# A wait for the project product between GpSimd's scatters

## The chip, the core and the metric

The kernel runs on one core of a Trainium2 chip. The metric is the device time of one execution in microseconds (us); three executions of the kernel before were timed. Every time that is read from a trace comes from one further, profiled execution.

## The reference

Per image, 14 x 14 patches are projected to 128 features, a class token and positions are added, and 128 text tokens are appended: 325 tokens of 128 features, for 128 images. On the layer-normed tokens runs an attention-like block (cumulative sums of phase-rotated values, written here as masked score products), whose result goes through a gate and the product with `Wo`, and is added back:

```
return x + total / norm @ Wo + bo
```

Then a second layer norm, and a mixture of experts: 64 experts, top 2 per token, at most 256 tokens per expert in order of arrival, and a shared expert beside them:

```
pos = cumulative count of the token's expert - 1
buf = zeros((E, CAP, d)).at[flat_e, pos].set(x_pairs, mode='drop')
y = silu(buf @ w1) * (buf @ w3) @ w2
return (shared + routed)
```

## The kernel before

The 128 images are worked on in 64 pairs. Each engine has its own program, written out in order: a loop over turns `k`, in which it does one stage of several pairs (`p1` is the pair of the turn before, `p2` the one before that, and so on). Semaphores count up once per pair and stage, and `wait_ge(S["pe_wo"], n)` waits until stage `pe_wo` has been done for `n` pairs. There is no scheduler: the order on an engine is the order of the calls in its `body(k)`, and the engine stands still while a wait is not met.

A pair goes through these steps, with the lines of the profile:

- TensorE (PE) makes the tokens (L919) and turns them over to rows; VectorE (DVE) takes their statistics and, in `scaled`, writes the variance `ve` (L1342). GpSimd (POOL) raises it to the power -1/2 in `rstd` (`rs`, L591). DVE's `bias_scale` waits for that and writes `nb` (L1348), with which ScalarE (ACT) normalizes both the new pair (`xh`, L739) and, for an earlier pair, the input of the second norm (`xs`, L726). One `rs` of 12 columns serves two pairs: six columns of the first norm of one pair, six of the second norm of the pair two before it.
- On DVE, behind `nb` in the same turn, stand the masks, the counts of the experts, the slots (`slot`, L1448, the row of `slot_rows` to which each token goes), and last `tot` (L1470), the gated sum.
- PE's `project` (L1078) is the first call of PE's next turn: it multiplies `tot` with `Wo` and counts up `pe_wo`. DVE's `second_rows` (L1499) waits for it and writes `h2`, from which the second norm's statistics are taken, which go into the same turn's `ve`.
- POOL scatters each token of a pair twice (top 2) to `slot_rows` in HBM, by 12 indirect DMAs (L605): `scatter(p8, part)` issues two for one of six parts. In its turn `k` it waits for the slots of pair `k - 8`, scatters parts 0 to 2, computes `rs` of pair `k - 4`, and scatters parts 3 to 5.

After the loop, the 64 experts run over what lies in `slot_rows`; SyncE (SP) waits for all scatters ahead of that. POOL then adds the results into `out_rows` (L639).

The turns of the engines are not in step by number. POOL's turn `k` holds `rs` of pair `k - 4`, whose variance DVE makes in its turn `k - 3`. The `project` of pair `k - 5` stands in PE's turn `k - 2`.

Of the kernel before, what the change touches and what calls it, by code (L numbers as in the profile page):

```python
# [141 lines left out]
def first(pair):  # L142
    return pair.c == 0


def steps(body, begin, end):

    for k in range(begin, PAIRS + end):
        body(Pair(k))
# [43 lines left out]
def expert_pairs(eng, body):  # L193

    for n in range(E // 2):
        body(Experts(n // 4, n % 4))


def wait_expert(eng, sem, pair, back=0, each=1):

    n = pair.number() + (1 - back)
    if not pair.fixed() or n > 0:
        eng.wait_ge(sem, n * each)
# [10 lines left out]
def program(nc, t, out, slots_d):  # L214
    ctx = ExitStack()
    with ctx:
# [3 lines left out]
        def sem(name):  # L220
            return ctx.enter_context(nc.semaphore(name))
# [7 lines left out]
        def cst(name, p=128):  # L229
            a, b = CONST[name]  # L230
            return const[0:p, a:b]
# [168 lines left out]
        S = {n: sem(n) for n in names}  # L400
# [13 lines left out]
        def first_columns(eng, n):  # L414

            b0, count = CHUNKS[n]
            return eng.tensor_copy(cols[:, b0:b0 + count, :], raw[:, 0, :].rearrange("p (t b) -> p b t", b=P)[:, b0:b0 + count, :])
# [155 lines left out]
        @block.gpsimd  # L573
        def _(pool):
            g = nc.gpsimd
            g.memset(neg_half[:, :], -0.5)
            g.memset(freq[:, :], 0.0).then_inc(s_pre_p, 1)
            pool.wait_ge(s_xin[0], 16 * 2 * C)
            first_columns(g, 2).then_inc(S["a_d2"], 1)
            g.memset(init_rows[:, :, 0:E_COL], 0.0).then_inc(s_pre_p, 1)  # L580
            g.memset(init_rows[:, :, E_COL:P_COL], -1.0)
            g.memset(init_rows[:, :, P_COL:T_COL], 0.0)
            pool.wait_ge(s_const, 16)
            g.tensor_copy(init_rows[:, :, T_COL], cst("empty")).then_inc(s_pre_p, 1)
            pool.wait_ge(s_pre_p, 3)

            def rstd(q):

                pool.wait_ge(S["v_ve"], q.count())
                half = 0 if q.runs() else 2 * NT  # L590
                g.tensor_tensor(out=rs[:, q.u, half:], in0=ve[:, q.u, half:], in1=neg_half[:, half:], op=ALU.pow).then_inc(S["p_rs"], 1)  # L591

            def ready(q):

                if first(q):
                    pool.wait_ge(s_init, 16 * (SLOTS // 1024 + 1))

                pool.wait_ge(S["v_slot"], q.count())

            def scatter(q, part):  # L600

                i = part % NT
                nt = TILES[i][1]
                for r in range(TOPK):
                    g.indirect_dma_start(  # L605
                        out=slots_d, out_offset=bass.IndirectOffsetOnAxis(
                            ap=slot[0:nt, q.x, r, part:part + 1], axis=0),
                        in_=xs[0:nt, q.x, part, :], in_offset=None, bounds_check=SLOTS - 1,
                        oob_is_err=False).then_inc(s_scat[q.x], 16)

            def body(k):
                p4 = k.back(4)
                p8 = k.back(8)
                if p8.runs():
                    ready(p8)
                    scatter(p8, 0)
                    scatter(p8, 1)
                    scatter(p8, 2)
                if p4.runs(BEHIND):
                    rstd(p4)  # L620
                if p8.runs():
                    scatter(p8, 3)
                    scatter(p8, 4)
                    scatter(p8, 5)
            steps(body, 4, 8)

            for u in range(2):
                pool.wait_ge(s_store[u], 16 * NT * (PAIRS // 2))
            pool.wait_ge(l_store, 16 * NT * len(LATER))

            last_row = pool.to_reg(TOKENS + SPARE - 1)

            def add(q):

                for e, ready in enumerate(("e_ya", "e_yb")):
                    wait_expert(pool, X[ready], q)
                    wait_expert(pool, e_add[e], q, 1, 32)
                    for m in (2 * e, 2 * e + 1):
                        g.indirect_dma_start(  # L639
                            out=out, out_offset=bass.IndirectOffsetOnAxis(ap=etok[:, q.load, m:m + 1], axis=0),  # L640
                            in_=ysum[:, q.load, m, :], in_offset=None, bounds_check=last_row,
                            compute_op=ALU.add).then_inc(e_add[e], 16)

            expert_pairs(pool, add)
            for e in range(2):
                pool.wait_ge(e_add[e], (E // 2) * 32)
# [1116 lines left out]
```

## Time and profile before

| what | value |
|---|---|
| three timed executions | 1828.45, 1853.2, 1863.95 us |
| their median | 1853.2 us |
| the profiled execution: first to last instruction | 1823.6 us |
| its own time outside of that span | not given; the lowest timed run is 4.85 us above the span, the median 29.6 us |
| PE, DVE, ACT, POOL busy | 1534.0, 1421.6, 1256.5, 1226.0 us |
| the loop, first `rs` behind a scatter to the last `rs` | 132.9 to 1514.8 us |
| scatters (L605) | 768 |

A busy time is the sum over an engine's instructions. The granted clock is 1.00 where TensorE had its full rate and 0.50 where it had half. "issue" as a releaser means that the trace shows nothing that the engine waited for, "remote" that the semaphore's update is seen later than the end that the trace has for any instruction that could have made it.

### The profile page before, as it was taken

What the parts mean: (1) busy time and instruction counts of PE and PEld (TensorE: products, weight loads), DVE (VectorE), ACT (ScalarE), POOL (GpSimd) and SP (SyncE); (2) the same over time, 40 slices, a digit from 0 to 9 for tenths busy, and PEclk for the clock granted to TensorE, in tenths of its full rate; (3) what the DMA queues carried; (4) which work ended last, traced back from release to release, by engine and by line L of the source; (5) the groups of instructions that cost most, each with busy time, mean ns of one, the idle gap of its engine ahead of it and who ended that gap; (6) DMA issues with size and microseconds to landing.
All of it is one profiled execution on the core that took longest, in us unless ns stands there. A gap on an engine that the chain in (4) does not pass through costs nothing.

```text
span 1823.6 us, 30829 instructions
## 1 busy us (share of the span) xinstructions
PE 1534.0 (84%) x9237; PEld 1158.6 (64%) x9237; DVE 1421.6 (78%) x5705; ACT 1256.5 (69%) x2195; POOL 1226.0 (67%) x973
## 2 busy tenths in 40 slices
PE   2888998999899999888989898999889975676672
PEld 1566776777676767656767666677667764554552
DVE  3477997999797988777888888889888975587661
ACT  2897997988788878777878787889878851111110
POOL 1025776777676767666667676777667767488887
PEclk9899999999999999999999999999999998899886
DMA  9965666666666666556555655566656221476653
GB/s 182 229 138 120 138 139 125 123 121 124 102 117 100 117 101 106 96 103 103 95 101 104 108 102 102 101 111 105 103 103 103 63 59 40 96 116 109 98 88 35
DMA packets 267117, 197.21 MB, mean 108 GB/s; under 512 B 65464, under 2 KB 246437, under 8 KB 266953
## 3 DMA queue, kind: packets, MB, share of 16 engines
q1 hardware_dynamic: 210120, 174.84, 50.2%
q0 software_dynamic: 51200, 17.87, 8.4%
q10 hardware_dynamic: 5633, 2.56, 0.7%
q8 instruction: 74, 1.21, 0.3%
q14 instruction: 90, 0.74, 0.2%
HBM read 86.24 MB, written 85.39 MB: 94 GB/s over the span
## 4 chain that ended last, share of the span: by engine, by line
PE 40%; ACT 22%; issue 11%; POOL 9%; another core or an unknown queue 8%; DVE 7%; DMA 3%; SPq 0%; ACTq 0%; POOLq 0%; DVEq 0%
POOL out_rows L639 6%; PE bank L919 5%; PE bank L999 5%; ACT img L656 5%; ACT xh L739 4%; PE bank L1087 3%; PE bank L982 3%; POOL slot_rows L605 3%; PE bank L946 2%; PE bank L1018 2%; PE bank L1078 2%; ACT xs L726 2%; ACT kq L793 2%; ACT kq L792 2%
## 5 line engine op out<-in xcount | busy, mean ns | idle before, releaser
L605 POOL DMA_INDIRECT slot_rows<-xs,slot x768 | 874.1, 1138 | 284.5 <-issue 247.3
L656 ACT ACTIVATE img<-img 84x980 f32<-84x980 f32 x190 | 339.6, 1788 | 14.8 <-DMA img<-in_x 7.2
L591 POOL TENSOR_TENSOR rs<-ve,neg_half 128x12 f32<-128x12 f32 (+1 forms) x66 | 150.3, 2277 | 234.4 <-DVE ve L1342 232.8
L919 PE MATMUL bank<-img,w_tok 126*128 126x392 f32 (+1 forms) x640 | 228.7, 505 | 27.9 <-DMA img<-img 23.3
L639 POOL DMA_INDIRECT out_rows<-img,etok x128 | 198.7, 1552 | 64.0 <-issue 35.0
L919 PEld LDWEIGHTS bank<-img,w_tok 126*128 126x128 f32 (+1 forms) x640 | 124.0, 195 | 113.3 <-issue 23.3
L982 PEld LDWEIGHTS bank<-pos_a,v 128*128 128x128 f32 x768 | 145.4, 198 | 54.0 <-issue 10.8
L982 PE MATMUL bank<-pos_a,v 128*128 128x325 f32 (+2 forms) x768 | 163.8, 351 | 6.1 <-issue 3.8
L726 ACT ACTIVATE xs<-h,nb,rs 128x128 f32<-128x128 f32 x384 | 154.0, 481 | 3.0 <-DVE nb L1348 3.0
L739 ACT ACTIVATE xh<-h,nb,rs 128x128 f32<-128x128 f32 x384 | 154.0, 480 | 1.3 <-DVE nb L1348 1.3
L1499 DVE TENSOR_TENSOR h<-bank,hbo 128x768 f32<-128x768 f32 x64 | 61.1, 955 | 114.6 <-remote 103.3
L999 PE MATMUL bank<-a_t,v 128*128 128x325 f32 (+2 forms) x768 | 149.9, 344 | 0.0
L999 PEld LDWEIGHTS bank<-a_t,v 128*128 128x128 f32 x768 | 126.4, 192 | 21.6 <-issue 0.4
L880 ACT ACTIVATE img<-bank 128x256 f32<-128x256 f32 x32 | 12.3, 384 | 174.0 <-PE bank L1191 129.2
L1219 PE MATMUL bank<-img,mate 128*128 128x128 f32 x504 | 77.2, 316 | 65.2 <-issue 65.2
L1219 PEld LDWEIGHTS bank<-img,mate 128*128 128x128 f32 x504 | 71.0, 225 | 72.2 <-issue 72.1
L1078 PEld LDWEIGHTS bank<-wo,tot 128*128 128x128 f32 x768 | 90.5, 191 | 32.0 <-issue 31.0
L1553 DVE TENSOR_TENSOR v<-bank,bv_row 128x768 f32<-128x768 f32 x64 | 61.2, 957 | 56.0 <-PE bank L1087 31.4
L766 ACT ACTIVATE lg<-bank 128x384 f32<-128x384 f32 x64 | 31.4, 491 | 104.7 <-remote 83.8
L1078 PE MATMUL bank<-wo,tot 128*128 128x128 f32 x768 | 102.7, 284 | 0.0
L960 PEld LDWEIGHTS bank<-kq 64*128 64x128 f32 x768 | 67.4, 186 | 53.7 <-issue 33.6
L1087 PE MATMUL bank<-wv,x_t 128*128 128x128 f32 x768 | 97.6, 277 | 0.8 <-ACT x_t L761 0.8
(217 smaller groups left out, 3697.1 us busy)
## 6 DMA issues: line engine op xcount, KB each, us to landing
img<-in_x SPq DMA_DIRECT2D x384, 150.1 KB
img<-img SPq DMA_DIRECT2D x254, 160.8 KB
img<-img SPq DMA_DIRECT2D x128, 128.6 KB
out_rows<-fin SPq DMA_DIRECT2D x128, 128.0 KB
slot_rows<-xs,slot POOLq DMA_INDIRECT x768
slot_rows<-init_rows SPq DMA_DIRECT2D x16, 540.0 KB, 9.1
img<-slot_rows SPq DMA_DIRECT2D x32, 270.0 KB
h<-in_txt SPq DMA_DIRECT2D x64, 128.0 KB
```

The lines of the kernel that those rows point to most:

```text
L591: g.tensor_tensor(out=rs[:, q.u, half:], in0=ve[:, q.u, half:], in1=neg_half[:, half:], op=ALU.pow).then_inc(S["p_rs"], 1)
L605: g.indirect_dma_start(out=slots_d, out_offset=bass.IndirectOffsetOnAxis(ap=slot[0:nt, q.x, r, part:part + 1], axis=0), in_=xs[0:nt, q.x, ...
L639: g.indirect_dma_start(out=out, out_offset=bass.IndirectOffsetOnAxis(ap=etok[:, q.load, m:m + 1], axis=0), in_=ysum[:, q.load, m, :], in_o ...
L656: a.activation(cols[:, b0:b0 + nb, :], raw[:, q.u, :].rearrange("p (t b) -> p b t", b=P)[:, b0:b0 + nb, :], ACT.Copy)\
L726: ins = a.activation(xs[:, z.x, i, 0:D], h2[:, z.u, i, :], ACT.Identity, bias=nb[:, m.u, 2 * NT + i:2 * NT + i + 1], scale=rs[:, m.u, 2 * ...
L739: ins = a.activation(xh[:, i, :], h[:, k.u, i // NT, i % NT, :], ACT.Identity, bias=nb[:, k.u, i:i + 1], scale=rs[:, k.u, i:i + 1])
L919: ins = mm(bank[:, 5, 0:2 * PATCHES], w_tok[r, m, :], xk[r, k.u, :, m, :], start=(m == 0), stop=(m == SHIFT - 1))
L982: ins = mm(bank[:, 6 + s, i * TILE:L], v[:, y.u, s, i, :], pos_a[:, BEGIN[i]:BEGIN[i + 1]], start=(i == 0), stop=(i == NT - 1))
L999: ins = mm(bank[:, 6 + s, i * TILE:L], v[:, y.u, s, i, :], flat[:, BEGIN[i]:BEGIN[i + 1]], start=(i == 0), stop=(i == NT - 1))
L1078: ins = mm(bank[:, s, i * D:(i + 1) * D], tot[:, s, t0:t0 + TILE], wo[:, :], start=True, stop=True)
L1087: ins = mm(bank[:, 4 + s, i * D:(i + 1) * D], x_t[:, s, t0:t0 + TILE], wv[:, :], start=True, stop=True)
L1219: ins = mm(bank[:, to, CAP + i * D:CAP + (i + 1) * D], mate[:, b, m, i * TILE:(i + 1) * TILE], ye[:, b, m, :], start=(m == 2 * e), stop=(m ...
```

## The change

In POOL's turn `k`, a wait is put between part 4 and part 5 of the scatters. It asks that `pe_wo` has counted the pair `k - 5`, that is, that PE has done `k - 4` products with `Wo`. Nothing is removed, and no engine's order of instructions changes.

```diff
             def body(k):
                 p4 = k.back(4)
+                p5 = k.back(5)
                 p8 = k.back(8)
                 if p8.runs():
                     ready(p8)
...
                 if p8.runs():
                     scatter(p8, 3)
                     scatter(p8, 4)
+                if p5.runs():
+                    pool.wait_ge(S["pe_wo"], p5.count())
+                if p8.runs():
                     scatter(p8, 5)
             steps(body, 4, 8)
```

POOL, start of the loop, in the kernel before (`rs` is the reciprocal root, `slot_rows` the table of the experts' inputs, a name behind "waits" a semaphore; x6 says that six such rows follow each other):

```order
L591 TENSOR_TENSOR rs<-ve,neg_half 128x12 [waits v_ve] x3
L605 DMA slot_rows<-xs,slot 16384x135 [waits v_slot,s_init]
L605 DMA slot_rows<-xs,slot 16384x135 x5
L591 TENSOR_TENSOR rs<-ve,neg_half 128x12 [waits v_ve]
L605 DMA slot_rows<-xs,slot 16384x135 x6
L605 DMA slot_rows<-xs,slot 16384x135 [waits v_slot]
```

The same place in the changed kernel:

```order
L591 TENSOR_TENSOR rs<-ve,neg_half 128x12 [waits v_ve]
L591 TENSOR_TENSOR rs<-ve,neg_half 128x12 [waits v_ve,pe_wo] x2
L605 DMA slot_rows<-xs,slot 16384x135 [waits v_slot,s_init,pe_wo]
L605 DMA slot_rows<-xs,slot 16384x135 x5
L591 TENSOR_TENSOR rs<-ve,neg_half 128x12 [waits v_ve]
L605 DMA slot_rows<-xs,slot 16384x135 x4
L605 DMA slot_rows<-xs,slot 16384x135 [waits pe_wo]
L605 DMA slot_rows<-xs,slot 16384x135
L605 DMA slot_rows<-xs,slot 16384x135 [waits v_slot]
```

The wait stands four scatters behind an `rs` and eight ahead of the next one: the two of part 5, and the six of parts 0 to 2 of the next turn. Turns 5 to 7, which have no scatters yet, get the wait too. It is there in 64 turns, 5 to 68; in 61 of them, 8 to 68, scatters stand behind it.

## Rows read from the trace of the kernel before

**Rows 1.** The page: busy time of each engine, share of the span, instructions.

```profile
PE 1534.0 (84%) x9237; PEld 1158.6 (64%) x9237; DVE 1421.6 (78%) x5705; ACT 1256.5 (69%) x2195; POOL 1226.0 (67%) x973
```

**Rows 2.** Groups by line, 132.9 to 1514.8 us: busy us, mean ns | idle before, releasers.

```profile
L605 POOL DMA_INDIRECT slot_rows<-xs,slot x732 | 834.6, 1140 | 259.7 <-issue 236.3 <-DVE slot L1448 23.4
L591 POOL TENSOR_TENSOR rs<-ve,neg_half 128x12 f32<-128x12 f32 (+1 forms) x62 | 141.1, 2276 | 147.8 <-DVE ve L1342 146.2 <-issue 1.2
L1499 DVE TENSOR_TENSOR h<-bank,hbo 128x768 f32<-128x768 f32 x61 | 58.2, 955 | 114.3 <-remote 103.3 <-PE bank L1078 11.0
```

**Rows 3.** Line L591: duration ns min/median/max, first and last start; then who waited.

```profile
L591 POOL TENSOR_TENSOR rs<-ve,neg_half x66: 1357/2303/2334, 43.1 to 1514.8; 128x12 f32<-128x12 f32 x64, 128x6 f32<-128x6 f32 x2
...
  DVE nb L1348: 4.5, 4
```

**Rows 4.** POOL by time: start us, us, engine, line, operation [idle before, releaser].

```profile
956.60 2.30 POOL L591 TENSOR_TENSOR rs<-ve,neg_half 128x12 f32<-128x12 f32 x1 [1.50 <-DVE ve L1342]
959.10 1.39 POOL L605 DMA_INDIRECT slot_rows<-xs,slot  x1 [0.20 <-issue]
...
965.54 1.00 POOL L605 DMA_INDIRECT slot_rows<-xs,slot  x1 [0.30 <-issue]
966.85 0.99 POOL L605 DMA_INDIRECT slot_rows<-xs,slot  x1 [0.30 <-issue]
968.50 0.97 POOL L605 DMA_INDIRECT slot_rows<-xs,slot  x1 [0.66 <-issue]
...
975.31 0.98 POOL L605 DMA_INDIRECT slot_rows<-xs,slot  x1 [0.30 <-issue]
979.58 2.30 POOL L591 TENSOR_TENSOR rs<-ve,neg_half 128x12 f32<-128x12 f32 x1 [3.28 <-DVE ve L1342]
```

**Rows 5.** DVE and PE by time, the same turn, and the next `nb`.

```profile
959.57 0.16 DVE L1348 SCALAR_TENSOR_TENSOR nb<-ms,rs 128x12 f32<-128x12 f32 x1
968.50 0.87 DVE L1470 TENSOR_TENSOR tot<-gsets,gpos 128x650 f32<-128x650 f32 x1
970.41 1.60 PE L1078 MATMUL bank<-wo,tot 128*128 128x128 f32 x12
974.32 0.96 DVE L1499 TENSOR_TENSOR h<-bank,hbo 128x768 f32<-128x768 f32 x1 [2.44 <-remote]
979.32 0.17 DVE L1342 TENSOR_SCALAR ve<-vs 128x12 f32<-128x12 f32 x1
...
982.55 0.16 DVE L1348 SCALAR_TENSOR_TENSOR nb<-ms,rs 128x12 f32<-128x12 f32 x1
```

**Rows 6.** Instructions (x) of L591, L605, L605, L1078 from the span's start.

```profile
0.00:957.00 957.00, 92.60 (x41) 0.97 0.65 123
0.00:957.00 957.00, 499.92 (x438) 0.97 0.65 123
0.00:971.00 971.00, 63.19 (x473) 55.77 (x474) 0.97 0.65 122
0.00:972.20 972.20, 64.20 (x480) 56.59 (x480) 0.97 0.65 122
```

**Rows 7.** POOL and DVE by time: an `nb` that waited for `rs`.

```profile
43.06 2.31 POOL L591 TENSOR_TENSOR rs<-ve,neg_half 128x12 f32<-128x12 f32 x1 [28.90 <-DVE ve L1342]
45.41 0.17 DVE L1348 SCALAR_TENSOR_TENSOR nb<-ms,rs 128x12 f32<-128x12 f32 x1 [2.50 <-POOL rs L591]
```

**Rows 8.** DVE and PE by time: the quickest and the slowest update shown.

```profile
665.51 1.60 PE L1078 MATMUL bank<-wo,tot 128*128 128x128 f32 x12
667.32 0.96 DVE L1499 TENSOR_TENSOR h<-bank,hbo 128x768 f32<-128x768 f32 x1 [0.35 <-PE bank L1078]
...
911.76 0.16 DVE L1348 SCALAR_TENSOR_TENSOR nb<-ms,rs 128x12 f32<-128x12 f32 x1
922.23 1.60 PE L1078 MATMUL bank<-wo,tot 128*128 128x128 f32 x12
929.58 0.96 DVE L1499 TENSOR_TENSOR h<-bank,hbo 128x768 f32<-128x768 f32 x1 [4.13 <-remote]
```

**Rows 9.** DVE and POOL by time: a scatter that waited for its slots.

```profile
945.86 0.17 DVE L1448 TENSOR_TENSOR slot<-slotf,over 128x12 int32<-128x12 f32 x1
946.80 0.97 POOL L605 DMA_INDIRECT slot_rows<-xs,slot  x1 [2.36 <-DVE slot L1448]
```

**Rows 10.** POOL by time, behind the loop: the first and last of eight scatters.

```profile
1541.53 0.97 POOL L605 DMA_INDIRECT slot_rows<-xs,slot  x1 [0.30 <-issue]
...
1550.91 0.97 POOL L605 DMA_INDIRECT slot_rows<-xs,slot  x1 [0.31 <-issue]
```

**Rows 11.** Stretches: PE, PEld, DVE, ACT, POOL busy (x), granted clock, DMA share, GB/s.

```profile
1541.00:1552.00 11.00, 2.55 (x17) 1.87 (x15) 0.00 (x0) 0.21 (x1) 8.45 (x9) 0.83 0.13 28
120.00:1430.00 1310.00, 1204.30 (x7186) 909.45 (x7185) 1112.56 (x4268) 1088.73 (x1905) 922.38 (x748) 0.99 0.61 110
926.00:930.00 4.00, 2.24 (x11) 1.59 (x10) 0.42 (x1) 0.76 (x2) 1.98 (x2) 1.00 0.84 149
930.00:934.00 4.00, 3.40 (x9) 2.58 (x10) 3.83 (x27) 3.97 (x8) 0.26 (x1) 0.57 1.00 120
1500.00:1560.00 60.00, 36.79 (x169) 27.51 (x169) 30.54 (x126) 10.98 (x25) 43.58 (x41) 0.80 0.16 36
```

## The prediction, as it stood before the result

> **What bounds the kernel now.** I read the page's busy times first [rows 1]: PE leads with 1534.0 us of 1823.6, DVE follows, and POOL, whose program alone changes, is busy for two thirds. That average hides what matters here, so next come the groups of the loop [rows 2]. From the first to the last of 62 `rs`, 132.9 to 1514.8 us, lie 61 turns, (1514.8 - 132.9) / 61 = 22.65 us each. POOL's scatters take 834.6 us in these turns and 259.7 us go by ahead of them, nearly all of it "issue"; with 141.1 us of `rs` that makes 1235.4 us, 20.25 us of each turn. POOL's only real slack is the 147.8 us ahead of `rs`, 2.4 us a turn. So POOL is nearly full, and `rs` is on time by little: DVE has waited for it only 4 times in the whole run, 4.5 us in total [rows 3].
>
> Then one turn by time. POOL's row [rows 4] is `rs` at 956.60, six scatters from 959.10, six more from 968.50, `rs` again at 979.58. DVE and PE [rows 5] show the ring that the pairs go round: `nb` at 959.57, `tot` at 968.50, `project` at 970.41, its update taken by `second_rows` at 974.32, `ve` at 979.32, and then `rs`. Now it is this ring and PE's own work that set 22.65 us; POOL's scatters lie beside it.
>
> **Which product is waited for.** By 957 us, 41 `rs` and 438 = 36 x 12 + 6 scatters have started [rows 6]. So the `rs` at 956.60 is that of turn 44, and 965.54 and 966.85 are its part 5. The wait there asks for 44 - 4 = 40 products, each 12 rows of L1078. At 971 there are 473 rows, at 972.2 there are 480 = 40 x 12 [rows 6]. The product asked for is the one at 970.41, of PE's *next* turn, and its update is seen at 974.32. Part 5 now starts 4.9 us before that product starts and 8.8 us before its update. The wait is not met when POOL reaches it, and POOL stands there.
>
> **What is queued behind it.** Two scatters of part 5, the six of parts 0 to 2, and then `rs`, all in order on POOL; DVE's `nb` waits for `rs`, and with `nb` all that follows on DVE, ACT and PE up to `tot` and the next `project`. So a new ring closes through POOL: `rs` -> `nb` -> `tot` -> `project` -> wait -> eight scatters -> next `rs`. Each turn must last at least as long as this ring. Its parts:
>
> - `rs` to `nb`: where DVE waited for it, 45.41 - 43.06 = 2.35 us [rows 7]. Now it is 2.97 (956.60 to 959.57), since DVE gets there later by itself; DVE will be early, so I take 2.35.
> - `nb` to `project`: 970.41 - 959.57 = 10.84 [rows 5], 922.23 - 911.76 = 10.47 [rows 8]. DVE needs to the end of `tot` at 969.37 for it, 9.80 us, so little can be won by PE and ACT being early. I take 10.7, with 10.0 as the lower end.
> - `project` to its update as DVE sees it: 1.81 at the quickest, 7.35 at the slowest [rows 8], 3.91 in the turn of rows 5. What delays it beyond PE's 1.60 us the trace does not say ("remote"). The 114.3 us that DVE idles ahead of `second_rows` are 1.87 us a turn [rows 2]; on top of the quickest 1.81 that gives 3.7. PE will have more room than now, which may free it of some of this. I take 2.9, between 1.8 and 3.8.
> - update to the first scatter: a scatter that waited for its slots starts 946.80 - 946.03 = 0.77 us after they end [rows 9]. DVE's own start already holds a little of the update's way; I take 0.7.
> - eight scatters: 965.54 to the end of the last, 976.29, is 10.75 us [rows 4]. Over the loop the twelve of a turn take (834.6 + 259.7 - 23.4) / 61 = 17.56 us, against 17.2 in this turn (959.10 to 976.29), so I take 11.0.
> - The next `rs` follows at once, because `ve` comes 5.0 us after the update [rows 5], and POOL comes 11.7 us after it.
>
> Sum: 2.35 + 10.7 + 2.9 + 0.7 + 11.0 = 27.65 us a turn, 5.0 more than 22.65. There are 61 turns with scatters behind the wait, the same 61 intervals: 61 x 5.0 = 305 us.
>
> **What costs nothing.** In turns 5 to 7 POOL has no scatters and waits for `ve` anyway, which comes behind the product's update. Behind turn 68 there is no wait, and the last 30 scatters run as now; the experts start behind them as now, later by the same 305 us. The DVE work between the update and `nb` (`h2`, statistics, indices) takes 982.55 - 974.32 = 8.2 us now and hides under POOL's 11.7 + 2.35. The buffers of the scattered rows come free up to 9 us later, but ACT uses them again only in the next turn or later.
>
> Made against the profiled execution, 1823.6 + 305 = 2129 us of span. The lowest timed run lies 4.9 us above the span, the median 29.6. Going by neither end: **2140 us**, 15% over the median of 1853.2.
>
> **A rule of the skill against the sum.** Behind the loop, with DVE at 0.00 us [rows 11], eight scatters take 1551.88 - 1541.53 = 10.35 us [rows 10] instead of 11.0, and `rs` varies only from 2303 ns at the median to 2334 at most [rows 3]. If the scatters got as quick with DVE waiting, the sum would be 0.65 us less a turn, 40 us in all; I leave it in the range, since DVE works on through two thirds of the eight scatters.
> The Trainium skill ("GPSIMD Engine Reference", Key points) says that GpSimd shares its SBUF interfaces with VectorE and contends with it in a 2-port mode or with two SBUF inputs. By that rule a waiting DVE makes POOL quicker, and the time would be nearer 2100.
>
> **The rivals.**
>
> 1. *The ring is shorter: the late updates go.* The update at 1.8, `nb` to `project` 10.0, scatters as behind the loop 10.35: 2.35 + 10.0 + 1.8 + 0.7 + 10.35 = 25.2, +156 us, 1985 with 5 us around it. It speaks for this that PE has backlog now and will not have it; against it that all three ends would have to meet. With one or two of them, 2030 to 2090. Chance 0.22 for all below 2080.
> 2. *TensorE's clock falls.* It is 0.99 in the loop with PE busy 1204.30 of 1310 us; 0.80 where it is busy 36.79 of 60; and after PE had stood still in 926 to 930 it was 0.57 in the next 4 us [rows 11]. PE's work in a turn is 1204.30 / 1310 x 22.65 = 20.8 us [rows 11], 75% of 27.65. If PE set the whole 10.7 us between `nb` and `project` and ran at 0.80, they would grow by a quarter, 2.7 us a turn, 163 us: 2300 at most, 2220 with half of that. Against it: PE's gaps now are not followed by a drop each time. Chance 0.15 for all above 2215.
> The Trainium skill ("TensorE: Matmul & The Clock Gate", What's actually happening) has the slow clock as the default that sustained work lifts; by that alone the drops would be regular.
> 3. *The wait costs nothing and the kernel is not slower.* It decides at the point where the product's update is earlier than POOL's arrival at part 5: then no `rs` is late. That holds if the ring to the update were 8.8 us shorter than in rows 4 and 5, or if the wait meant the product one turn earlier; then the time is 1853. If besides, scatters held back let PE's updates through in time, the 103.3 "remote" us go: 1750. The counts of rows 6 speak against the first, the 2.4 us of slack against the second. Chance 0.04: 0.03 no change, 0.01 faster.
>
> The forecast's own case has 0.59. Slower by over 2% are the forecast and the first two rivals, 0.96. (About 2% is what a measurement of this kernel can tell from no change.) The likeliest time is 2140. The range goes from 2035 (ring at 26.0) to 2230 (ring at 28.8 and 30 us around it, or a small loss of clock).
>
> **What would show it.** In the changed kernel's trace: at part 5 POOL idles some 7.7 us a turn (2.35 + 10.7 + 2.9 + 0.7 after the start of `rs`, where it could go on after 965.54 - 956.60 = 8.94), released by L1078; the 147.8 us ahead of `rs` go to nearly nothing; DVE waits for `rs` at L1348 in nearly every turn; `rs` to `rs` is 27 to 28 us; the scatters' count and mean stay. It would be wrong if POOL's new idle time is there but ahead of `rs` some slack is left: then another ring is longer. It would be wrong from the start if part 5 goes on without idle time.

## The result, and the profile after

The changed kernel takes 2110.4 us at the median of four runs (2109.8 to 2112.6), the kernel before 1857.4 in the same comparison (1828.5 to 1864.0): a ratio of 1.144, 95% interval 1.135 to 1.153. The forecast was 2140 us, between 2035 and 2230, and slower. The profiled execution took 2111.0 us, 2108.9 of them in the span, 2.1 outside.

The page of the changed kernel answers to [rows 1], busy time and share of the span:

```profile
PE 1618.7 (77%) x9237; PEld 1256.6 (60%) x9237; DVE 1439.1 (68%) x5705; ACT 1259.4 (60%) x2195; POOL 1180.6 (56%) x973
```

No engine has more instructions to do, all stand still for longer; PE's busy time is 85 us up with the same 9237 products, at a lower clock (below). The groups of the loop, 135.4 to 1798.8 us (busy us, mean ns | idle us before, releasers), answer to [rows 2]:

```profile
L605 POOL DMA_INDIRECT slot_rows<-xs,slot x733 | 789.9, 1078 | 733.0 <-PE bank L1082 535.4 <-issue 197.5
L591 POOL TENSOR_TENSOR rs<-ve,neg_half 128x12 f32<-128x12 f32 (+1 forms) x62 | 142.9, 2305 | 0.4
L1503 DVE TENSOR_TENSOR h<-bank,hbo 128x768 f32<-128x768 f32 x61 | 58.4, 957 | 13.2 <-PE bank L1082 13.2
```

L1082 is `project`, L1503 `second_rows` (four lines further down than before). POOL waits 535.4 us for the product. The 147.8 us of slack ahead of `rs` have become 0.4. DVE's idle time ahead of `second_rows` has fallen from 114.3 to 13.2 us, and nothing in it is "remote" any more. Who waits for `rs`, in the view of line L591, answers to the 4.5 us of [rows 3]:

```profile
L591 POOL TENSOR_TENSOR rs<-ve,neg_half x66: 1373/2321/2663, 43.4 to 1798.8; 128x12 f32<-128x12 f32 x64, 128x6 f32<-128x6 f32 x2
...
  DVE nb L1352: 276.4, 64
```

61 turns take (1798.8 - 135.43) / 61 = 27.27 us each, where they took 22.65. One of them on POOL, in order of time, as in [rows 4]:

```profile
1009.15 2.34 POOL L591 TENSOR_TENSOR rs<-ve,neg_half 128x12 f32<-128x12 f32 x1
1011.67 1.04 POOL L605 DMA_INDIRECT slot_rows<-xs,slot  x1 [0.19 <-issue]
...
1016.02 1.17 POOL L605 DMA_INDIRECT slot_rows<-xs,slot  x1 [0.30 <-issue]
1026.24 0.99 POOL L605 DMA_INDIRECT slot_rows<-xs,slot  x1 [9.04 <-PE bank L1082]
...
1035.63 0.98 POOL L605 DMA_INDIRECT slot_rows<-xs,slot  x1 [0.30 <-issue]
1036.62 2.32 POOL L591 TENSOR_TENSOR rs<-ve,neg_half 128x12 f32<-128x12 f32 x1
```

Four scatters, 9.04 us of standing still, eight scatters, and `rs` at once. The same turn on DVE and PE, as in [rows 5]:

```profile
1011.52 0.17 DVE L1352 SCALAR_TENSOR_TENSOR nb<-ms,rs 128x12 f32<-128x12 f32 x1 [4.44 <-POOL rs L591]
...
1013.31 0.55 PE L973 MATMUL bank<-both,below 128*128 128x448 bf16 x1 [3.73 <-DVE two L1386]
...
1014.31 2.91 PE L950 MATMUL bank<-sw,su 128*128 128x128 f32 x12
...
1021.66 0.84 DVE L1474 TENSOR_TENSOR tot<-gsets,gpos 128x650 f32<-128x650 f32 x1
...
1023.84 1.60 PE L1082 MATMUL bank<-wo,tot 128*128 128x128 f32 x12
...
1025.48 0.96 DVE L1503 TENSOR_TENSOR h<-bank,hbo 128x768 f32<-128x768 f32 x1 [0.18 <-PE bank L1082]
...
1029.41 0.38 DVE L1346 TENSOR_SCALAR ve<-vs 128x12 f32<-128x12 f32 x1
```

The ring can be read off: `rs` 1009.15, `nb` 1011.52, `project` 1023.84, its update 1025.48, first scatter 1026.24, next `rs` 1036.62. `ve` was there 7 us before POOL took it up. In the same turn the granted clock goes down and comes back. In these rows it is the third number from the end, and PE's busy time is the first sum:

```profile
1009.00:1011.40 2.40, 0.57 (x10) 0.43 (x6) 0.00 (x0) 1.02 (x1) 2.40 (x2) 0.92 0.07 6
1011.40:1013.50 2.10, 0.19 (x1) 0.13 (x2) 1.98 (x8) 1.78 (x5) 1.61 (x3) 0.50 0.01 0
1013.50:1017.00 3.50, 3.50 (x17) 3.20 (x16) 3.50 (x10) 2.95 (x8) 2.89 (x3) 0.50 0.02 1
1017.00:1020.00 3.00, 3.00 (x20) 2.75 (x19) 2.67 (x10) 1.20 (x2) 0.20 (x1) 0.86 0.18 49
1020.00:1023.60 3.60, 3.60 (x31) 2.88 (x30) 2.57 (x4) 2.24 (x2) 0.00 (x0) 1.00 0.61 164
```

### The profile page after: what moved, and what is told of

It is laid out like the page before. It is cut to its first block, busy times and chain, and to the rows that moved or that the text cites. A ratio compares the mean times of both kernels' runs of the same rounds, so it can differ in the third digit from the quotient of the medians.

```text
span 2108.9 us, 30831 instructions
## 1 busy us (share of the span) xinstructions
PE 1618.7 (77%) x9237; PEld 1256.6 (60%) x9237; DVE 1439.1 (68%) x5705; ACT 1259.4 (60%) x2195; POOL 1180.6 (56%) x973
## 4 chain that ended last, share of the span: by engine, by line
PE 38%; POOL 26%; issue 23%; DVE 5%; ACT 3%; DMA 2%; another core or an unknown queue 1%; POOLq 1%; SPq 0%; ACTq 0%; DVEq 0%
POOL slot_rows L605 13%; PE bank L950 7%; POOL out_rows L643 7%; PE bank L1003 7%; POOL rs L591 6%; PE bank L1082 5%; PE bank L1091 4%; PE bank L1098 2%; PE bank L1067 2%; PE bank L939 2%; DVE su L1490 2%; PE bank L1022 2%; PE bank L1045 2%; PE bank L973 2%; PE bank L979 1%
## 5 line engine op out<-in xcount | busy, mean ns | idle before, releaser
L605 POOL DMA_INDIRECT slot_rows<-xs,slot x768 | 827.1, 1077 | 762.0 <-PE bank L1082 553.7
L973 PE MATMUL bank<-both,below 128*128 128x448 bf16 x64 | 34.9, 546 | 232.0 <-DVE two L1386 229.4
L591 POOL TENSOR_TENSOR rs<-ve,neg_half 128x12 f32<-128x12 f32 (+1 forms) x66 | 152.0, 2304 | 86.3 <-DVE ve L1346 85.9
L1352 DVE SCALAR_TENSOR_TENSOR nb<-ms,rs 128x12 f32<-128x12 f32 (+1 forms) x66 | 11.2, 170 | 276.4 <-POOL rs L591 276.4
L950 PE MATMUL bank<-sw,su 128*128 128x128 f32 x708 | 168.4, 427 | 0.0
L964 PE MATMUL bank<-kq 64*128 64x325 f32 (+2 forms) x768 | 91.0, 371 | 91.5 <-ACT sl L758 59.1
L964 PEld LDWEIGHTS bank<-kq 64*128 64x128 f32 x768 | 75.2, 198 | 137.7 <-issue 128.2
L950 PEld LDWEIGHTS bank<-sw,su 128*128 128x128 f32 x708 | 155.3, 328 | 0.6
L986 PE MATMUL bank<-pos_a,v 128*128 128x325 f32 (+2 forms) x768 | 155.1, 339 | 0.0
L973 PEld LDWEIGHTS bank<-both,below 128*128 128x128 bf16 x64 | 6.7, 104 | 241.8 <-DVE two L1386 238.9
L758 ACT ACTIVATE sl<-bank 128x650 f32<-128x650 f32 x59 | 42.0, 712 | 161.7 <-remote 150.8
```

Source lines behind the costliest of these rows:

```text
L605: g.indirect_dma_start(out=slots_d, out_offset=bass.IndirectOffsetOnAxis(ap=slot[0:nt, q.x, r, part:part + 1], axis=0), in_=xs[0:nt, q.x, ...
L950: ins = mm(bank[:, 4 + s, i * D:(i + 1) * D], su[:, s, t0:t0 + TILE], sw2[:, :], start=True, stop=True)
L964: ins = mm(dst, kq[r, y.u, 0, t0:t0 + TILE], kq[r, y.u, 1, i * TILE:L], start=(i < 2), stop=(i != 1), skip_group_check=True)
L986: ins = mm(bank[:, 6 + s, i * TILE:L], v[:, y.u, s, i, :], pos_a[:, BEGIN[i]:BEGIN[i + 1]], start=(i == 0), stop=(i == NT - 1))
```

## The experiments

The theory: the ring through the product's update and eight scatters sets the turn, because `rs` is queued behind them. The rivals: the wait instruction itself, the lateness of the scatters (their traffic, their buffers), POOL's idle time as such, TensorE's clock.

These kernels ran on three chips, numbered here by the kernel before beside them: on chips A and C it takes 1663.8 and 1663.5 us, on chip B 1840.3. The comparison of the result ran on a chip that gave 1857.4. A ratio holds for its chip.

**The product of one turn earlier (chip A).**

```diff
-                p5 = k.back(5)
+                p6 = k.back(6)
...
-                if p5.runs():
-                    pool.wait_ge(S["pe_wo"], p5.count())
+                if p6.runs():
+                    pool.wait_ge(S["pe_wo"], p6.count())
```

> The wait at the same place asks for the product of pair k-6, one turn earlier, which POOL should find done. Theory (the ring through the product and eight scatters sets the turn): no scatter idles for L1082, the turn is 22.6 us as before, time within 1% of before (1835 to 1875). Rival (the wait instruction itself, or the split of the twelve scatters, costs): 61 waits at up to 0.7 us, 1890 or more.

Measured: 1662.9 us, ratio 0.999 (0.998 to 1.000). The time expected was the 1857 of the first chip; against the kernel before on its own chip it is the same. The wait costs nothing where it is met. The two groups of this kernel's page show something else as well:

```profile
L605 POOL DMA_INDIRECT slot_rows<-xs,slot x768 | 875.0, 1139 | 274.0 <-issue 263.4 <-DVE slot L1452 10.6
L1503 DVE TENSOR_TENSOR h<-bank,hbo 128x768 f32<-128x768 f32 x64 | 61.2, 957 | 12.4 <-PE bank L1082 12.1
```

Ahead of `second_rows` 12.4 us are idle, not 114, and none is "remote": with the same program, this chip has no late updates. Its 61 turns take (1362.0 - 132.14) / 61 = 20.16 us, so the 22.65 of [rows 2] held some 2.5 us a turn of a delay that is not in the program. It sits in the update of `project`: from the start of `project` to `second_rows` it is 1.64 or 1.65 us here in each of the 61 turns, and 4.16 in the mean of the turns of the first trace.

**Six or twelve scatters behind the wait (chip A).** The wait is put behind part 5, or ahead of part 3.

```diff
                 if p8.runs():
                     scatter(p8, 3)
                     scatter(p8, 4)
-                if p5.runs():
-                    pool.wait_ge(S["pe_wo"], p5.count())
-                if p8.runs():
                     scatter(p8, 5)
+                if p5.runs():
+                    pool.wait_ge(S["pe_wo"], p5.count())
```

> The same wait, put behind part 5: six scatters stand between it and rs instead of eight. Theory: the ring loses two scatters, 10.38 to 7.8 us, so the turn goes from 27.3 to 24.7 us and the time to 2109 - 61 x 2.6 = 1950; if TensorE's clock stays up with the shorter idle time, nb to project falls from 12.1 to 10.7 and it is 1865. Rival (what costs is that the traffic of part 5 comes late): part 5 is on time again, so the time is that of before.

> The same wait, put ahead of part 3, right behind rs: twelve scatters stand between it and the next rs. Theory: the ring grows by four scatters, 5.7 us, the turn is 33 us, time 2109 + 61 x 5.7 = 2455. Rival (POOL's own idle time at the wait is the cost, so it matters only how long it stands): POOL stands still from the end of rs instead of from 6 us later, which it could do for nothing if scatters were not queued behind; the time stays near 2110.

Measured: 1935.6 us with six (ratio 1.163, 1.160 to 1.166), where 1950 was expected, and 2459.6 with twelve (1.478, 1.475 to 1.481), where it was 2455. The view of line L591, with the first and the last start of `rs`, for the kernel with six scatters behind the wait:

```profile
L591 POOL TENSOR_TENSOR rs<-ve,neg_half x66: 1372/2321/2336, 41.5 to 1631.9; 128x12 f32<-128x12 f32 x64, 128x6 f32<-128x6 f32 x2
```

The same view for the kernel with twelve, with the idle time of `nb` behind `rs` (us, times):

```profile
L591 POOL TENSOR_TENSOR rs<-ve,neg_half x66: 1373/2321/2337, 43.0 to 2159.0; 128x12 f32<-128x12 f32 x64, 128x6 f32<-128x6 f32 x2
...
  DVE nb L1351: 740.5, 64
```

With the `rs` of turn 8 at 134.72 and 136.35, a turn is 24.54 us with six scatters behind the wait, 27.27 with eight (the trace of the result, another chip), 33.16 with twelve: 1.37 us for each of the first two, 1.47 for each of the next four, against some 1.3 for one scatter and its gap in the rows of the turn above. The cost goes by the number of scatters in the ring. In the mean of the turns they take 7.98, 10.46 and 16.14 us; most of the rest is that `nb` to `project` grows with them, 11.83, 12.05 and 12.27. With six of them part 5 comes on time, and the kernel is still 16% slower, so it is not the late traffic of part 5.

**Part 5 a turn later, with no wait (chip A).**

```diff
+                p9 = k.back(9)
...
                 if p4.runs(BEHIND):
                     rstd(p4)
+                if p9.runs():
+                    scatter(p9, 5)
                 if p8.runs():
                     scatter(p8, 3)
                     scatter(p8, 4)
-                    scatter(p8, 5)
-            steps(body, 4, 8)
+            steps(body, 4, 9)
```

> The kernel before without any wait, but part 5 of each pair is scattered a turn later, right behind the next rs. The two scatters come some 17 us later than before, later than in the changed kernel, and no update is waited for. Theory (only rs queued behind the wait costs): time as before, 1835 to 1875. Rival (late scatters cost by themselves, through the buffers that they hold or the traffic that they meet): as in the changed kernel, 2000 or more.

Measured: 1665.4 us, ratio 1.001 (1.000 to 1.002). Two scatters a turn that come later cost nothing here. (Again the times expected were those of the first chip; the ratio is what answers.)

**The changed kernel again (chip B).**

> The changed kernel beside the kernel before on the chip of the experiments. The kernel before took 1664 us in the first experiments, not 1857, so its late updates are not part of the program. Theory (the ring hides what delays the updates, 1.64 us from project to second_rows in every turn): the changed kernel takes 2109 us here too, and the ratio is 2109 / 1664 = 1.27, not 1.14. Rival (the chip of the first pair was slower throughout): it is about 1664 x 1.144 = 1903.

Measured: 2114.7 us beside 1840.3, ratio 1.149 (1.140 to 1.157). Chip B turned out to be of the kind of the first one, so this repeats the result and does not decide between theory and rival; g below does.

**PE kept busy ahead of the counts (chip B).** The changed kernel and

```diff
                 if p4.runs():
+                    for _ in range(12 if p2.runs() else 0):
+                        tr(bank[:, 0, 0:TILE], ident, ident)
                     counts(p4)
```

> The changed kernel; ahead of counts, where PE idles 3.7 us a turn for nb's followers, PE does 12 transposes of a constant into the free bank 0. Theory (1.4 us of the 12.1 between nb and project are TensorE's half clock after that idle time): the granted clock stays near 1.00, nb to project falls to 10.7, 61 x 1.4 = 85 us less than the changed kernel. Rival (PE's chain is longer for another reason): the clock rises but nb to project stays at 12, or the 12 transposes add their 3.3 us: 2110 to 2310.

Measured: 2068.8 us, 46 less than the changed kernel beside it. The groups of L950, the first float32 products behind the idle time, on the page of the changed kernel beside it and then with the filler:

```profile
L950 PE MATMUL bank<-sw,su 128*128 128x128 f32 x708 | 168.1, 426 | 0.0
```

```profile
L950 PE MATMUL bank<-sw,su 128*128 128x128 f32 x708 | 117.8, 329 | 0.0
```

The loop's stretch in the profile of the changed kernel shown first (another chip), then in that with the filler (columns as in [rows 11], the granted clock being the third number from the end):

```profile
135.40:1798.80 1663.40, 1346.28 (x7526) 1053.38 (x7525) 1189.03 (x4492) 1129.14 (x1985) 930.35 (x795) 0.87 0.51 88
```

```profile
140.00:1740.00 1600.00, 1380.85 (x8226) 1088.26 (x8227) 1178.47 (x4455) 1125.84 (x1979) 922.21 (x785) 0.94 0.51 91
```

The clock rises from 0.87 to 0.94. More work made the kernel quicker, so the half clock is a real part of what the change costs: 46 us at least. The 85 expected did not come, and the clock came to 0.94, not near 1.00. In the mean of the 61 turns `nb` to `project` fell from 12.03 us in the kernel beside it to 11.17, not to 10.7. How much of the other 39 us is the clock and how much the filler's own time stays open; at a clock of 1.00 in every turn, a_one_earlier has 11.30 us from `nb` to `project`, so not all of what lies above 10.7 need be the clock.

**`rs` taken off POOL (chip B).** DVE makes `rs` behind `top_indices`, by a reciprocal; the results' scale is another, the order of all other work is not. The changed kernel (i) and the kernel before (j) both get

```diff
                 if p4.runs(BEHIND):
-                    rstd(p4)
...
+            def root(q):
+                dve.wait_ge(S["v_ve"], q.count())
+                half = 0 if q.runs() else 2 * NT
+                vv.reciprocal(rs[:, q.u, half:], ve[:, q.u, half:]).then_inc(S["p_rs"], 1)
...
                 if p4.runs():
                     top_indices(p4)
+                if p1.runs(BEHIND):
+                    root(p1)
```

> The changed kernel with its wait, but rs is made on DVE (a reciprocal in place of the power -1/2, so the norms' scale is another) and POOL only scatters. Theory (the wait costs because rs is queued behind it): POOL still idles for L1082, the 12 scatters and the wait fit into a turn (17.6 + 0.8 us of 20.1), and the time is that of the kernel before on the same chip within 2%. Rival (the wait costs by holding scatters or their buffers back): as the changed kernel, 1900 to 2110.

> The control for that: the kernel before, with rs made on DVE in the same way and no wait. Theory: the same time as with the wait, within 1%, and the kernel before plus at most 61 x 0.2 = 12 us for DVE's extra instruction, or less by what DVE waited for POOL.

Measured: 2269.9 us with the wait, 2082.1 without it (ratios 1.232 and 1.134). Both expectations failed: the control is 13% over the kernel before, and the wait costs 188 us though no `rs` is behind it. The token sum `h_t` shows what its idle time waits for, in i and then in j:

```profile
L1361 DVE TENSOR_TENSOR h_t<-bank,pos_t 128x392 f32<-128x392 f32 x64 | 36.3, 568 | 318.4 <-remote 298.4 <-PE bank L921 14.2 <-issue 5.8
```

```profile
L1357 DVE TENSOR_TENSOR h_t<-bank,pos_t 128x392 f32<-128x392 f32 x64 | 36.1, 564 | 109.9 <-remote 90.0 <-PE bank L917 15.2 <-issue 4.7
```

It waits for the update of PE's token product long after the trace has that product done. The kernels of chip A have no "remote" wait at all. Either the lateness of scatters costs after all, or this is the chip's late updates, which grew. That called for the same pair where updates are not late.

**The same with small image loads (chip C).** From the third pair on each load fetches one of 14 rows of patches, in four kernels: the kernel before (f), the changed one (g), and both with `rs` on DVE (k with the wait, l without).

```diff
+                        if q.c > 1:
+                            src, dst = src[:, 0:1], dst[:, 0:1]
                         sp.dma_start(dst, src).then_inc(s_xin[q.u], 16)
```

> The kernel before, but from pair 2 on each image load fetches 1 of 14 rows of patches, so the tokens are made of stale pixels; the order of all instructions stays. Theory (the semaphores' updates are late, on some chips, while the image loads and scatters keep the DMA engines full, and that is what made the kernel before 1840 to 1857 us on two chips and 1664 on a third): about 1664 or a little less, 1630 to 1680, on any chip, with no remote waits. Rival (the late updates have nothing to do with the loads): 1840 on a chip where the kernel before takes 1840.

> The changed kernel with the same small loads. Theory (its ring, rs to project to wait to eight scatters, lies outside the late updates): 2100 to 2115 as with full loads, so that the change costs 2109 / 1664 = 1.27 once the kernel before is free of late updates. Rival (late updates are in its 27.3 us too): it falls by as much as the kernel before does, to 1930 or less.

> The wait with rs made on DVE (a reciprocal in place of the power -1/2), and the small loads. With full loads this took 2270 us against 2082 without the wait, both with late updates of up to 9 us. Theory (the wait costs through rs; those 188 us were later updates, since the twelve scatters then met the image loads): as the kernel l beside it, within 1%, near 1660. Rival (late scatters cost by themselves): 5% or more above l.

> The control: no wait, rs on DVE, small loads. Theory: as f, 1630 to 1690; the 240 us that rs on DVE added with full loads are late updates and go with the loads. Rival (moving rs, or the other scale, costs by itself): 1850 or more.

| kernel | time, us | ratio to the kernel before, 1663.5 us | interval |
|---|---|---|---|
| f, before | 1656.7 | 0.995 | 0.993 to 0.997 |
| g, with the wait | 2098.7 | 1.261 | 1.259 to 1.263 |
| l, `rs` on DVE, before | 1656.8 | 0.995 | 0.993 to 0.997 |
| k, `rs` on DVE, with the wait | 1659.6 | 0.998 | 0.997 to 0.999 |

This is the experiment that decides. All four came as the theory had them (g 1.3 us below its range), and none of them has a "remote" wait. With the same wait at the same place, moving `rs` off POOL takes 439 us away and leaves 3. And POOL still waits in k, as its list of waits shows (us, times, longest):

```profile
POOL slot_rows L607 <- PE bank L1082: 230.7, 61, 5.4
```

231 us of standing still in 61 turns, for 3 us of time, because nothing that anyone needs soon is queued behind it. The same view of g:

```profile
POOL slot_rows L607 <- PE bank L1084: 557.7, 62, 18.3
DVE nb L1354 <- POOL rs L593: 386.1, 64, 6.4
```

g against f is 442 us, 27%, by the program alone, and its turn is 27.27 us again. What k does not show is that the wait is free where updates are late: on chip B, with full loads, i took 188 us more than j. Since chip C gives the kernel before 1663.5 us with full loads too, f does not say whether the image loads make the updates late on the other chips.

## Why the prediction was right

**Which product, and whether POOL waits.** Right. POOL waited 61 times in the loop for L1082, and one product earlier it did not wait to any cost. The new idle time was 9.0 us in the turn shown and 8.8 in the mean (535.4 / 61), where 7.7 were forecast.

**The ring.** Right as a mechanism, shown by the number of scatters in it (24.54, 27.27, 33.16 us) and by k. By its terms:

| term | forecast, us | in the turn shown, us | mean of the 61 turns, us |
|---|---|---|---|
| `rs` to `nb` | 2.35 | 1011.52 - 1009.15 = 2.37 | 2.35 |
| `nb` to `project` | 10.7 | 1023.84 - 1011.52 = 12.32 | 12.05 |
| `project` to its update | 2.9 | 1025.48 - 1023.84 = 1.64 | 1.64 |
| update to first scatter | 0.7 | 0.76 | 0.76 |
| eight scatters | 11.0 | 1036.62 - 1026.24 = 10.38 | 10.46 |
| sum | 27.65 | 27.47 | 27.27 |

The sum is 0.4 us off, but three of its terms are mis-sized by more, and the errors cancel; that the time came within 30 us of the forecast is in part luck. `nb` to `project` was forecast 1.35 us too short in the mean, and a good part of that was my second rival. PE idles 3.73 us ahead of L973, the granted clock is 0.50 until past 1017, and the twelve products of L950 take 2.91 us where twelve of L1078 took 1.60 at the full clock. I had given that a chance of 0.15 and put it above 2215. It came in every turn: in none of the 61 is the clock above 0.86 between `nb` and `project`. The 1.35 us are 82 us in all, which is the half price for which I had named 2220; the time stayed below because the update and the scatters came out shorter by 77 and 33 us. The filler gave 46 of the 82 back. My reason against this rival, that PE's gaps before were not followed by a drop each time, was taken from a loop in which PE had hardly any gap, and I read one row too strongly: in 926 to 930 PE did not stand still but was busy for 2.24 of 4 us [rows 11].

The update's term is 1.26 us too long. In [rows 8] it took up to 7.35 us, here 1.64 in every turn. The late updates have not gone, they lie elsewhere. On the changed kernel's page ACT's `sl`, which waits for a product, idles for them, in the turn shown from 1032.1 to 1034.9:

```profile
L758 ACT ACTIVATE sl<-bank 128x650 f32<-128x650 f32 x59 | 42.0, 712 | 161.7 <-remote 150.8
```

POOL's eight scatters cover that stretch: the turn is 27.27 us in g too, where no update is late.

The scatters are 0.54 us quicker in the mean than I took them; 0.25 of that I had added myself to the 10.75 of [rows 4]. 10.46 is close to the 10.35 that they take behind the loop [rows 10], with DVE at rest. I had forecast that their mean stays; it went from 1140 ns to 1078. DVE idles more, but that this is the cause is not shown. Single scatters speak against it as the whole cause:

```profile
1028.82 0.97 POOL L605 DMA_INDIRECT slot_rows<-xs,slot  x1 [0.30 <-issue]
1031.38 1.17 POOL L605 DMA_INDIRECT slot_rows<-xs,slot  x1 [0.30 <-issue]
1033.48 0.17 DVE L1366 TENSOR_TENSOR xs<-topi,const 128x12 f32<-128x12 uint32 x1 [2.56 <-remote]
```

The one at 1028.82 took 0.97 us with DVE at work, the one at 1031.38 took 1.17 while DVE stood still, from 1030.92 to 1033.48.
The Trainium skill ("GPSIMD Engine Reference", Key points) says that GpSimd shares its SBUF interfaces with VectorE and can contend with it there; the mean of the trace moved the way that this would give, these two scatters did not.

**The median of the runs.** The span of 2108.9 and 2.1 us around it gave 2111; the 29.6 us that the median before lay above its span had no counterpart. It goes with the late updates: the runs of the kernel before differ by up to 1.9% on the two chips that have them, and by up to 0.5% on the two that have none. The cause of the spread is not shown.

**The rivals.** That the ring is shorter came true for two of its three ends and was offset by the clock. That the wait costs nothing was wrong, and a_one_earlier shows that the point from which it decides was rightly put: one product earlier it is free.

**What stays open.** Why semaphore updates come late in two of the four comparisons (the first and chip B). It is not the program's order alone (chips A and C run it without), and it matters for the size: 14 to 15% there, 26% in g. The changed kernel with full loads was not run on a chip without late updates; b and c were, on either side of it. The growth of the late updates in i and j is seen but not explained, and so it is not shown that later scatters are free on such a chip.

## What to carry to other kernels

The engine with the wait was busy only two thirds of the time, and yet the wait cost 14 to 27%, paid by what was queued behind it. So find the next instruction there that another engine needs, add up what stands between, and close the ring. The slack to compare with is the idle time ahead of that instruction, here 2.4 us, and not the engine's idle share. On chips without late updates, scatters as late or later cost nothing once the one short instruction behind them had left the queue (k), or did not stand behind a wait (d).

## What the runs showed of the hardware

- The same kernel took 1664 us on two chips and 1840 and 1857 in two other comparisons, with the granted clock hardly a reason for it: 0.956 in the profile at the first chip, 0.966 with a_one_earlier on chip A. The difference goes with "remote" waits, 103.3 us ahead of one DVE instruction [rows 2] against none. The turns differ by 2.49 us (22.65 and 20.16), and the time from the start of `project` to `second_rows` by 2.52 (4.16 and 1.64).
- While PE stood still for 3.73 us in a turn, the granted clock fell to 0.50 (1.2 of 2.4 GHz). It was there from 1011.4 us, 1.9 before PE went on, to 1017 at least, 3.7 behind that. The 128-column float32 products of L950 took 426 ns in the mean of the whole changed kernel, and 329 with the filler. Twelve useless transposes a turn gave 46 us back.
- The scatter behind the wait starts 0.76 to 0.77 us after DVE's `second_rows`, which waits for the same update, in all 61 turns, and one scatter follows another after 0.30 us in the turn shown. The eight take 10.46 us in the mean.
